# A gated cross-attention block: weight maxima taken in the attention loop, pairs weighed jointly, W_in's second half turned in another bank

## The reference

```python
    def _L0_xattn_ref(q, kv_src, seg_id, Wq, Wkv, Wo):
        qh = _split_heads(q @ Wq.T)
        kv = kv_src @ Wkv.T
        k, v = jnp.split(kv, 2, axis=-1)
        gather = seg_id[:, :, None] - offsets
        k_sel = kh[b_idx, :, gc].transpose(0, 3, 1, 2, 4)
        v_sel = vh[b_idx, :, gc].transpose(0, 3, 1, 2, 4)
        scores = jnp.einsum('bhqd,bhqkd->bhqk', qh, k_sel) * SCALE
        probs = jax.nn.softmax(scores, axis=-1)
        out = jnp.einsum('bhqk,bhqkd->bhqd', probs, v_sel)
        return out @ Wo.T
    def _L0_ffn_ref(x, W_in, b_in, W_out, b_out):
        hidden = jax.nn.gelu(x_sim @ W_in_sim + b_in, approximate=False)
        out = hidden_sim @ W_out_sim + b_out
    x = x + jnp.tanh(g_xattn[0]) * _L0_xattn_ref(_layernorm(x, axis=-1), ctx_1024, itok_BxS_0_511, L0_xattn_Wq, L0_xattn_Wkv, L0_xattn_Wo)
    x = x + jnp.tanh(g_ffn[0]) * _L0_ffn_ref(_layernorm(x, axis=-1), L0_ffn_W_in, L0_ffn_b_in, L0_ffn_W_out, L0_ffn_b_out)
```

## Time and profile before

| | |
|---|---|
| median of 3 runs | 311.67 us (310.97 to 313.34) |
| the profiled execution | 311.57 us, its span 309.4 us |
| busy share of the span: PE, DVE, ACT, POOL | 91%, 89%, 82%, 54% |
| chain that ended last | PE 49%, POOL 21%, DVE 18% of the span |
| mean granted TensorE clock | 0.989 |

### The profile page before, as it was taken

How to read it: one execution, slowest core, us unless ns; L and a number is a source line. 1 busy time by engine, 2 the same in 40 slices (tenths; PEclk the granted TensorE clock), 3 DMA queues, 4 the chain that set the end, 5 groups by cost and what they waited for, 6 DMA issues and landing times.

```text
span 309.4 us, 6195 instructions
## 1 busy us (share of the span) xinstructions
PE 281.3 (91%) x1946; PEld 214.1 (69%) x1946; DVE 276.0 (89%) x523; ACT 252.2 (82%) x514; POOL 165.7 (54%) x144
## 2 busy tenths in 40 slices
PE   6999999999997898998985669999999899999991
PEld 5776787887876787887783534444444688888881
DVE  0899999999999999999989883999998799999991
ACT  2789899899897896788761867999999699999980
POOL 1136899989998799999998203233335001111110
PEclk9999999999999999999999989999999999999997
DMA  7993210000000000000000001013111004444446
GB/s 208 335 407 122 65 51 22 0 2 2 0 3 0 1 2 0 2 0 3 1 1 2 0 0 68 3 78 126 68 68 68 2 0 67 72 68 68 68 68 138
DMA packets 7606, 17.46 MB, mean 56 GB/s; under 512 B 1414, under 2 KB 3918, under 8 KB 7198
## 3 DMA queue, kind: packets, MB, share of 16 engines
q1 hardware_dynamic: 5167, 12.80, 11.3%
q0 software_dynamic: 1008, 3.67, 7.8%
q10 hardware_dynamic: 1407, 0.69, 0.8%
HBM read 7.82 MB, written 7.86 MB: 51 GB/s over the span
## 4 chain that ended last, share of the span: by engine, by line
PE 49%; POOL 21%; DVE 18%; issue 5%; ACT 3%; DMA 2%; ACTq 0%; DVEq 0%; POOLq 0%
PE bank L1043 18%; PE bank L1010 18%; POOL vsel L357 10%; POOL vsel L360 7%; DVE prod L1116 4%; PE bank L830 4%; PE bank L810 3%; DVE bank L1122 3%; POOL o L364 3%; PE bank L788 2%; DMA bin_ld<-in_L_ffn_b_in_dram 2%; POOL rstd L348 1%; POOL both_rstd L345 1%; DVE xres L1172 1%; ACT xn L481 1%
## 5 line engine op out<-in xcount | busy, mean ns | idle before, releaser
L810 PE MATMUL bank<-kvtab,onehot 80*128 80x256 f16 x512 | 64.9, 273 | 5.9 <-ACT vsel L496 3.3
L357 POOL TENSOR_TENSOR vsel<-vsel,pr 128x1024 f32<-128x1024 f32 x31 | 59.9, 1933 | 8.6 <-DVE pr L1152 8.6
L810 PEld LDWEIGHTS bank<-kvtab,onehot 80*128 80x128 bf16 x512 | 48.6, 97 | 18.8 <-ACT vsel L496 5.2
L690 ACT ACTIVATE hidden<-bank,bin__58,zscale 128x512 f32 x64 | 47.8, 789 | 3.8
L1010 PE MATMUL bank<-xhi,win 128*128 128x512 f16 x128 | 49.4, 386 | 1.2 <-ACT win L410 1.2
L1010 PE MATMUL bank<-xlo,win 128*128 128x512 f16 x128 | 49.3, 385 | 0.0
L1478 DVE SCALAR_TENSOR_TENSOR hlo<-hq,rel_wout,hhi 128x512 f16<-128x512 int16 x64 | 45.6, 742 | 0.0
L1422 DVE TENSOR_REDUCE hmax<-hidden (+1 forms) x31 | 36.3, 1213 | 7.4 <-ACT hidden L690 7.0
L360 POOL TENSOR_TENSOR vsel<-vsel 128x512 f32<-128x512 f32 x31 | 39.4, 1273 | 2.4
L389 POOL TENSOR_TENSOR xres<-xres,bout 128x1024 f32<-128x1024 f32 x8 | 18.8, 2358 | 38.8 <-DVE xlo L1417 38.8
L1116 DVE TENSOR_TENSOR prod<-bank,q 128x1024 f32<-128x1024 f32 x32 | 38.8, 1213 | 0.8 <-PE bank L810 0.8
(11 more groups left out here) (165 smaller groups left out, 499.8 us busy)
## 6 DMA issues: line engine op xcount, KB each, us to landing
out_dram<-xres SPq DMA_DIRECT2D x7, 512.0 KB, 2.6
out_dram<-y POOLq DMA_DIRECT2D x7, 512.0 KB, 5.4
xres<-in_x_dram SPq DMA_DIRECT2D x3, 1024.0 KB, 16.5
onehot<-onehot SPq DMA_DIRECT2D x9, 160.0 KB, 2.6
xres<-in_x_dram SPq DMA_DIRECT2D x2, 512.0 KB, 7.0
win_ld<-in_L_ffn_W_in_dram SPq DMA_DIRECT2D x1, 1024.0 KB, 12.8
wout_ld<-in_L_ffn_W_out_dram SPq DMA_DIRECT2D x1, 1024.0 KB, 20.7
wkv_ld<-in_L_xattn_Wkv_dram SPq DMA_DIRECT2D x1, 512.0 KB, 5.2
```

What stands on the lines that cost most here:

```text
L357: pool.tensor_tensor(v3, v3, pr[k][:, t].rearrange("p o h -> p (o h)").unsqueeze(2).broadcast_to([P, KW * H, HD]), ALU.mult).then_inc(s_pv, 1)
L690: act.activation(hidden[:, g, f, :], bank, ACT.Gelu, bias=bin_[:, f:f + 1], scale=zscale[:, f:f + 1]).then_inc(s_h, 1)
L810: mm = pe.matmul(dst[:, off * D:(off + 1) * D], onehot[0:U, off, bass.ds(tile * P, P)], kvtab[:, b, part, col:col + D], start=(part == 0), ...
```

## The change

Each half of W_in is no longer reduced behind the loop: in steps 8 to 15 PE turns one chunk f of W_in (`win_chunk`, 2 transposes) into the bank of the attention output, DVE takes its maximum into one column of `peak_win` beside a column that POOL has filled with the floor, and the scales are made in step 16. W_out's floor goes the same way, and its scaling and diagonal go to ACT. POOL weighs both tiles of a pair with each instruction, in two buffers of a pair in place of four of a tile. In PE's loop the transposes of `o` stand ahead of the second gathers; orders on ACT and DVE change, and behind the loop on all engines. `win_back` of the second half writes to bank23 ahead of the feed-forward. The core of the diff:

```diff
-        vsel = [a_r.put(f"vsel{i}", [P, KW, D], F32) for i in range(4)]
+        vsel = [a_r.put(f"vsel{i}", [P, 2, KW, D], F32) for i in range(2)]
...
+        win_back_to = [ps_w, bank23[:, 512:1024]]
+        WIN_AT = {8: 0, 9: 1, 10: 2, 11: 3, 12: 4, 13: 5, 14: 6, 15: 7}
...
-            def weigh_v(u, k, t):
-                n = 2 * u + t
-                v = vsel[n % 4]
-                v3 = v[:].rearrange("p o (h d) -> p (o h) d", h=H)
-                pool.wait_ge(s_vc2, n + 1)
+            def weigh_pair(u, k):
+                nt = 2 if u < NP - 1 else 1
+                v = vsel[k][:, 0:nt]
+                pool.wait_ge(s_vc2, 2 * u + nt)
                 pool.wait_ge(s_p, u + 1)
-                pool.tensor_tensor(v3, v3, pr[k][:, t].rearrange("p o h -> p (o h)").unsqueeze(2).broadcast_to([P, KW * H, HD]),
-                                   ALU.mult).then_inc(s_pv, 1)
-                pool.wait_ge(s_pv, n + 1)
-                pool.tensor_tensor(v[:, 0:2, :], v[:, 0:2, :], v[:, 2:4, :], ALU.add).then_inc(s_pv2, 1)
-                pool.wait_ge(s_pv2, n + 1)
+                v3 = v.rearrange("p t o (h d) -> p (t o h) d", h=H)
+                pool.tensor_tensor(v3, v3, pr[k][:, 0:nt].rearrange("p t o h -> p (t o h)").unsqueeze(2)
+                                   .broadcast_to([P, nt * KW * H, HD]), ALU.mult).then_inc(s_pv, 1)
+                pool.wait_ge(s_pv, u + 1)
+                pool.tensor_tensor(v[:, :, 0:2, :], v[:, :, 0:2, :], v[:, :, 2:4, :], ALU.add).then_inc(s_pv2, 1)
+                pool.wait_ge(s_pv2, u + 1)
                 if first(u, 2):
                     pool.wait_ge(s_oTp, u - 1)
-                pool.tensor_tensor(o[k][:, t, :], v[:, 0, :], v[:, 1, :], ALU.add).then_inc(s_o, 1)
+                pool.tensor_tensor(o[k][:, 0:nt, :], v[:, :, 0, :], v[:, :, 1, :], ALU.add).then_inc(s_o, 1)
...
+                if hf == 0:
+                    act.wait_ge(s_wilev, 1)
+                    act.activation(sc_win[:], sc_win[:], ACT.Copy, scale=W_LEVELS).then_inc(s_winsc, 1)
+                    act.wait_ge(s_winsc, 1)
+                act.wait_ge(s_winTp, hf + 1)
...
+            def wout_scales():
+                act.wait_ge(s_wlev, 2)
+                act.wait_ge(s_ident, 2)
+                act.activation(sc_wout[:], sc_wout[:], ACT.Copy, scale=W_LEVELS).then_inc(s_woutsc, 1)
+                act.activation(diag[:], ident[:], ACT.Copy, scale=top_wout[:, 0:1]).then_inc(s_wrow, 1)
+            def wout_ratio():
+                act.wait_ge(s_wtop, 1)
+                act.activation(rel_wout[:], amax_wout[:], ACT.Copy, scale=top_wout[:, 2:3]).then_inc(s_rel, 1)
             def round_wout(m):
+                if m == 0:
+                    wout_scales()
...
-                if first(n, 4):
-                    act.wait_ge(s_o, n - 3)
-                act.activation(vsel[n % 4][:].rearrange("p o d -> p (o d)"), ps_v[:], ACT.Copy,
+                if first(u, 2):
+                    act.wait_ge(s_o, u - 1)
+                act.activation(vsel[u % 2][:, t].rearrange("p o d -> p (o d)"), ps_v[:], ACT.Copy,
...
                 if on(1):
                     copy_v(i - 1, 0)
+                if on(4) and on_act(i - 4):
+                    sums2(i - 4, k)
+                if i in SECOND1:
+                    sums1(SECOND1[i])
+                if on(3):
+                    evac_oT(i - 3, 1 - k)
+                if on(5):
+                    norm2(i - 5, 1 - k)
+                if on(4) and on_act(i - 4):
+                    squares2(i - 4, k)
                 if on(0):
                     evac_q(i, k)
...
-            ROUND_AT = {10: 0, 11: 1, 12: 2, 13: 3, 14: 4, 15: 5}
+            ROUND_AT = {9: 0, 10: 1, 12: 2, 13: 3, 14: 4, 15: 5}
...
+            evac_xn2T(NP - 5, 1)
             exp(NP - 1, 1)
-            evac_xn2T(NP - 5, 1)
+            round_win(0)
             evac_oT(NP - 2, 0, ps_w)
             norm2(NP - 4, 0)
             var_eps(NP - 3, 1)
-            round_win(0)
+            half_win(0)
             evac_oT(NP - 1, 1, ps_q)
             norm2(NP - 3, 1)
+            evac_xn2T(NP - 4, 0)
             var_eps(NP - 2, 0)
-            evac_xn2T(NP - 4, 0)
-            half_win(0)
+            round_win(1)
             norm2(NP - 2, 0)
-            var_eps(NP - 1, 1)
             evac_xn2T(NP - 3, 1)
             norm2(NP - 1, 1)
-            evac_xn2T(NP - 2, 0)
-            round_win(1)
             half_win(1)
             keep_win8(0)
+            act.wait_ge(s_tanh, 1)
+            act.activation(bout[:], bout[:], ACT.Copy, scale=tanhs[:, 1:2]).then_inc(s_bias, 1)
+            evac_xn2T(NP - 2, 0)
+            evac_xn2T(NP - 1, 1)
             keep_win8(1)
-            evac_xn2T(NP - 1, 1)
+            wout_ratio()
...
+            def win_chunk(i):
+                pe.wait_ge(s_win, 16)
+                pe.wait_ge(s_x1, i - 3)
+                f = WIN_AT[i]
+                for c in range(C):
+                    mm = pe.transpose(ps_y[:, c * P:(c + 1) * P], win_ld[:, c, f * P:(f + 1) * P], ident[:])
+                mm.then_inc(s_wmT, 1)
             def attn_out(u, k):
+                if u + 3 in WIN_AT:
+                    pe.wait_ge(s_wmax, WIN_AT[u + 3] + 1)
+                if u + 3 == NP:
+                    pe.wait_ge(s_wtop, 1)
...
+                if i in WIN_AT:
+                    win_chunk(i)
+                if i == NP:
+                    pe.wait_ge(s_const, 3)
+                    pe.wait_ge(s_x1, NP - 3)
+                    spread(ps_y[:, 0:P], s_wrow, s_wall)
                 if on(0):
                     queries(i, k)
+                if on(3):
+                    transpose_o(i - 3, 1 - k, (s_xn2T, i - 5) if on(6) else (s_oh, SEG_AT[i] + 2) if i in SEG_AT else (s_kvlo, NB) if i in KV_AT and KV_AT[i] == NB - 1 else (s_xT, i + 1))
                 if on(1):
                     gather_k(i - 1, 1)
-                if on(3):
-                    transpose_o(i - 3, 1 - k, (s_xn2T, i - 5) if on(6) else (s_oh, SEG_AT[i] + 2) if i in SEG_AT else (s_kvlo, NB) if i in KV_AT and KV_AT[i] == NB - 1 else (s_xT, i + 1))
...
+            transpose_xn2(NP - 5, 1, (s_oT, NP - 2))
             pe.wait_ge(s_win, 16)
             pe.wait_ge(s_prod, 2 * NP)
             win_T(0)
-            transpose_xn2(NP - 5, 1, (s_oT, NP - 2))
             pe.wait_ge(s_q, NP)
             idle_work(ps_q[:, P:4 * P], 10, 3)
             pe.wait_ge(s_q, NP)
             idle_work(ps_q[:, P:4 * P], 10, 3)
+            transpose_o(NP - 2, 0, (s_p, NP), ps_w)
             pe.wait_ge(s_q, NP)
             idle_work(ps_q[:, P:4 * P], 10, 3)
-            pe.wait_ge(s_q, NP)
-            spread(ps_q[:, 0:P], s_wrow, s_wall)
-            transpose_o(NP - 2, 0, (s_p, NP), ps_w)
             attn_out(NP - 2, 0)
-            transpose_xn2(NP - 4, 0, (s_xn2T, NP - 4))
+            pe.wait_ge(s_winq, 1)
+            idle_work(bank01[:, 0:512], 6)
             pe.wait_ge(s_lastpv, 1)
             win_T(1)
-            pe.wait_ge(s_rel, 1)
+            pe.wait_ge(s_wtop, 1)
             transpose_o(NP - 1, 1, (s_q, NP), ps_q)
+            transpose_xn2(NP - 4, 0, (s_xn2T, NP - 4))
             attn_out(NP - 1, 1)
-            transpose_xn2(NP - 3, 1, (s_xn2T, NP - 3))
+            pe.wait_ge(s_oT, NP - 1)
+            idle_work(ps_w, 8)
             pe.wait_ge(s_oT, NP - 1)
             win_back(0)
+            pe.wait_ge(s_winq, 1)
+            idle_work(bank01[:, 0:512], 6)
+            transpose_xn2(NP - 3, 1, (s_xn2T, NP - 3))
+            pe.wait_ge(s_winq, 1)
+            idle_work(bank01[:, 0:512], 6)
+            pe.wait_ge(s_winq, 1)
+            idle_work(bank01[:, 0:512], 6)
             transpose_xn2(NP - 2, 0, (s_xn2T, NP - 2))
-            pe.wait_ge(s_x1, NP)
-            idle_work(ps_y, 4)
             pe.wait_ge(s_x1, NP)
             idle_work(ps_y, 4)
             pe.wait_ge(s_oT, NP)
             spread(ps_q[:, 0:P], s_xall, s_qxr)
+            win_back(1)
             pe.wait_ge(s_x1, NP)
             idle_work(ps_y, 4)
             transpose_xn2(NP - 1, 1, (s_xn2T, NP - 1))
+            pe.wait_ge(s_x1, NP)
+            idle_work(ps_y, 4)
...
-                        pe.wait_ge(s_x1, NP)
-                        win_back(1)
+                    if isinstance(g, int) and g == 0 and f == 3:
+                        pe.wait_ge(s_w8, 2)
...
-                pw = prod[1][:].rearrange("p o d -> p (o d)")
-                dve.scalar_tensor_tensor(out=pw.rearrange("p (h d o) -> p o h d", h=H, o=KW),
-                                         in0=ps_v[:].rearrange("p (o h d) -> p o h d", o=KW, h=H), scalar=kvs[:, 1, NB - 1:NB],
-                                         in1=pr[k][:, 1].unsqueeze(3).broadcast_to([P, KW, H, HD]),
+                dve.scalar_tensor_tensor(out=prod[1][:].rearrange("p o (h d) -> p (o h) d", h=H),
+                                         in0=ps_v[:].rearrange("p (n d) -> p n d", d=HD), scalar=kvs[:, 1, NB - 1:NB],
```

(46 more changed lines are left out.)

102 lines of the change are left out of this document (40 added, 62 removed).

## The result

The changed kernel takes 302.14 us (median of 4 runs, 301.98 to 302.38) beside 312.50 for the kernel before (4 runs, 310.97 to 313.60): a ratio of 0.967, 95% interval 0.962 to 0.972. The ratios here compare only executions within 1.5% of the fastest of their own kernel, so they need not be quotients of medians. The direction was right, the size was not: 9.6 us were saved between the two profiled executions (311.57 and 301.99) and 10.4 between the medians, where I had worked out 5.9.

The account below looks back on a forecast made before the run. DVE and POOL were both taken as full in the attention loop. From 311.57 us, 4.6 for the earlier last residual and 1.3 from there to the ninth feed-forward matmul were subtracted, giving 305.7, range 303.2 to 308.8.

Parts of the forecast that it names:

- DVE in the loop: Attention loop on DVE: new maxima +2.6, step 9 -2.75, step 14 -0.2, together -0.3 us.
- The line between gives 0.41: Steps 8 to 15: a 128x256 reduce read between two known sizes, 0.33 us each after overlap, 2.6 for eight.
- a DVE step of 9.15: Sign that the forecast is right: DVE steps 10 to 13 of the loop take 9.15 us each.
- Step 9: Loop step where W_out's diagonal and scaling on DVE wait for POOL; giving them to ACT saves 2.75 us.
- The early steps: Loop steps 3 and 5: transposes of o ahead of the gather lengthen DVE's wait, +0.7 us, bounds 0 and 1.3.
- Pairs weighed jointly: POOL in the loop: a pair weighed with joint instructions takes 7.45 us in place of 8.1.
- rival (c): POOL in the loop becomes the bound and the kernel slower, 320 us at a pair of 9.4; chance 0.06.
- a pair of 8.05: POOL in the loop: the time per jointly weighed pair from which POOL would be late again.
- The tail: Behind the loop: last o transposed at 167.4 in place of 171.96, last residual 4.6 us earlier; PE's queue ends last.
- Entry: Last residual to ninth feed-forward matmul: -1.2 us from PE at its 2.4 GHz level and -0.1 from scaling b_out.
- Start, rest and what lies outside the span: Before pair 0's second-tile qk, after the ninth feed-forward matmul, and outside the span: forecast 20.07, 122.3 and 2.2 us.

Follow-up runs that it names:

- e1: The changed kernel with the loop order of before for DVE's second half of a step: 305.18 us, ratio 0.977 to the kernel before.
- e12: The changed kernel with the last o transposed ahead of W_in's second half, and pair 12's xn2 transposes behind the last attention output: 303.22 us, ratio 0.968.
- e15: e12 with POOL's power for pair 12 also moved behind its last half of the weighing, and bias, norm 2 and maximum later: 303.43 us, ratio 0.970.

## Why the prediction was wrong in size

**The step that failed is "DVE in the loop".** "The line between gives 0.41", less the overlap "0.33 each", measured 0.32, and "DVE has no gap in it" held in steps 10 to 13. But the forecast of "a DVE step of 9.15" priced the added instruction and left out the reorder that the diff made beside it (aggregate between product and sum, largest between sum and mask): a term put at nothing without a reason. The step took 8.89. Undone alone the reorder is 1.95 us, and the loop then takes 132.30 where the forecast had 132.7. Step 9, expected at 9.7, took 9.23 and with the old order 9.50.

**The early steps** were over-charged: +0.7, of which the trace shows 0.4 at the start of step 6 (40.72 us behind the end of *start*, 40.34 before). With DVE's old order (e1) it is 0.5, and the run with the gather first shows 0.25 for PE's order alone. The waits were as said (0.47 at 56.05). The bounds held, and the transposes' place repays it late in the loop.

**Step 9**: right in its mechanism and nearly in its first size (2.97 alone in the kernel before, 2.75 forecast). That it is worth 5.6 once POOL's instructions are long, 4.7 by the longer lock and most of the rest by PE's clock, had not been said: I wrote that the longer lock does not change the sum, which held only because both parts change together.

**Pairs weighed jointly**: 7.45 us exactly, rival (c) false. Its threshold, "a pair of 8.05", came out a little low: pair 14 starts on time while 63.7 + 10 + 10 pairs is at most 155.06, so up to 8.14. **The tail**: 4.87 of the forecast 4.9, but with a wrong reason for what ends last, which e12 showed to be POOL, tied with PE's queue. The sum for the last half on POOL had been 167.2 and for PE 167.4, so the time did not suffer. **Entry**: 1.31 of 1.3, and leaving the idle work out showed its cause.

**Start, rest and what lies outside the span**, 1.4 us of the miss together, belong to the executions, not to the change. In the rest the kernel before spent 122.30 us in its profiled execution, and 120.9 to 121.6 was measured in all seventeen others, three of them variants of before. Its last store, of 256 KB, landed 4.7 us after its issue, and the changed kernel's 3.7; in the three variants of before it was 3.2 to 3.8. A forecast against one execution inherits such luck. Had these stages come out as in that execution, the time would have been about 303.4, just inside the range, with the loop's error as large as it is.

Undone singly, the parts are worth 1.95 (order), 1.5 (joint), 5.6 (levels), 4.8 (maxima), 1.3 (idle work) and 2.1 (PE's order): 17 us where 9.6 were gained. Each leans on the others: the singly undone parts do not add up. The longer POOL instructions, for one, are only good with the levels gone from DVE.

## What to carry to other kernels

Price a reorder even if nothing is added: on a full DVE, look at the start-to-start distance of each pair in which the second reads the first, and put an independent instruction between (0.12 to 0.15 us each here), but only one whose own inputs are ready, and only while no other engine's step is as long. Before an instruction on POOL is made longer, look for DVE instructions beside it that end when POOL's do, however small, and move those first. A long stall on DVE can be paid a second time: where PE then stood for 3.98 and 4.88 us, its clock fell and the next step was longer too, by 0.75 and 1.4 us. When engines are equally full, forecast each part with the others in place, since alone it may be worth nothing, or the reverse.

## What was not expected of the hardware

The start comes in two lengths: 19.8 to 20.3 us in eleven of the profiled executions and 21.7 to 22.1 in seven, the changed kernel's variants in both groups, though no edit touches it. PE's timelines show it at its 8 transposes of W_kv and the 11 idle ones behind them. First the changed kernel run again, then e15, with the same instructions:

```profile
6.79 1.09 PE L796 MATMUL bank<-ident,wkv_ld 128*128 128x128 f32 x8
7.72 1.36 PE L772 MATMUL bank<-ident 128*128 128x128 f32 x11
```

```profile
6.88 1.97 PE L798 MATMUL bank<-ident,wkv_ld 128*128 128x128 f32 x8
8.63 2.37 PE L774 MATMUL bank<-ident 128*128 128x128 f32 x11
```

They take nearly twice as long, as at the 1.2 GHz level, though the granted clock reads 1.00 in both. All seven long starts show it (1.97 and 2.25 to 2.55 us), and none of the eleven short ones (1.09 and 1.36). So the rows show the slowing and leave its cause open. It is as large as most effects studied here, which is why stages and not medians carry the verdicts.
